# A two-layer transformer kernel: fp32 projections as three fp16 products, and feed-forward units of 256 tokens

## The chip, the cores and the metric

The kernel runs on one core of one Trainium2 chip. The metric is the time of one execution in device microseconds; the median of the runs shown stands for the kernel. All else is read from one profiled execution.

## The reference

Two layers act on x, [8, 256, 512] in fp32, so 8 batches of 256 tokens.

```python
xn = layernorm(x)
x = x + L0_attn(xn, Wqkv, Wo) + L0_ffn(xn, A, B, Wr)
xn = layernorm(x)
x = x + L1_attn(xn, Wq, bq, Wk, bk, Wv, bv) + L1_ffn(xn, gate_wq, ..., down_scale)
```

- L0_attn: 32 query heads of 16, one shared key and value head, scores with a linear bias by distance, a causal mask and softmax over 256 keys; the result times Wo (512 x 512).
- L0_ffn: four low-rank experts of rank 16; a softmax over the two largest of four gate logits mixes `xn @ A_e.T @ B_e.T`.
- L1_attn: inside each token. q is 16 x 32, k and v are 16. `scores[d, e] = sum over h of q[d, h] * k[e] * scale`, softmax over e, times v, and the 16 results are broadcast over 32 heads.
- L1_ffn: `down(silu(gate(x)) * up(x))`, 512 to 1792 to 512, with integer weights and a scale per output row.

## The kernel before

**Order.** The kernel is written step by step for each engine, and a planner in Python sets the order in which each engine meets its steps. `plan()` adds steps such as `("q", c, m)` with what they depend on; `Plan.run` simulates the engines with costs from the table `US` and takes, among the steps that could start first, the one with the lowest rank of the table `RANK` (a base and an amount per chunk). The resulting order is fixed in the program; on the chip only semaphores decide when a step starts. PSUM has eight banks in three kinds, A (2), B (4) and E (2), and each kind's banks are used in turn, so a step waits until the step that used the bank before has been read.

**Layer 0.** Tokens are taken in four chunks c of 512 (two batches i each). Per chunk: `ln0` and `xn0` normalise, `xT0` turns x by matmuls against an identity, `tok` makes keys, values and the low-rank products (fp32, 100 columns), `q` the queries in four tiles of 128x512 (fp32). ScalarE makes an fp16 high part of the queries, VectorE the low one, and both go through memory (`q_parts`) into `qq`. Then per batch: `max` (TensorE scores, VectorE maxima, 21 groups whose names carry i), `nm` (the maxima as rows of the operand), `exp` (8 head groups g of three tiles: TensorE scores, ScalarE exponentials L809 and L810, low halves by POOL L733 and VectorE L1244), `pv`, `attT` (turned attention output), `out` (Wo and the experts' second factor, five fp32 matmuls of 512 columns per 128 tokens, L983).

**Layer 1.** Per chunk of 512 tokens: `ln1`, `xn1`, `xT1` (turned x as fp16 high and low), `tok1`, the small attention `att1` to `att4` on VectorE, then 14 tiles of `gate` and `up` (8 matmuls of 512 columns each, L1014), ScalarE's tanh, VectorE's two products, the fp16 high part by ScalarE and the low by POOL (L745), and per 128 tokens `half` and `down` (28 matmuls of 512 columns, L1035).

**Side work.** POOL issues the late loads (`late`: Wo, lora_b, the weights of layer 1), and the feed-forward weights (`ffn_load`); its library call `partition_all_reduce` (L727) serves the maximum of a weight scale. SP issues the loads of x, the gathers and the stores.

The first `gate` step, behind the score groups of batch 3, divides the program: layer 0 of chunks 0 and 1 stands ahead of it, and the feed-forward fills TensorE behind it.

## Time and profile before

| | us |
|---|---|
| Median of 3 runs | 668.33 |
| Lowest and highest | 667.57, 668.47 |
| The profiled execution | 666.2 |
| Its span, first to last instruction | 664.4 |
| TensorE busy | 620.2 (93%) |
| VectorE busy | 454.2 (68%) |
| ScalarE busy | 349.8 (53%) |
| POOL busy | 284.2 (43%) |

A share is an average over stages with different limits. TensorE's mean granted clock is 0.969 of full speed. PE is TensorE, PEld its weight loads, DVE VectorE, ACT ScalarE and POOL GpSimd. An fp32 matmul leaves two records in the trace, an fp16 matmul one. Matmuls overlap, so the distance between starts tells more than the duration of one. "issue" is time in which an engine waited for nothing that the profile shows.

### The profile page before, as it was taken

The page shows a single profiled execution, that of the slowest core. Times are in us where ns is not written, and L with a number is a line of the kernel's source. Part 1 is how long each engine was busy: PE and PEld are TensorE (multiplying, and loading weights), DVE is VectorE, ACT ScalarE, POOL GpSimd, SP SyncE. Part 2 cuts the span into 40 slices and gives each one's busy share as a digit, 9 for nine tenths or more (in the row PEclk, how much of TensorE's full clock was granted, in tenths as well). Part 3 has the DMA queues.
Part 4 walks back from the last instruction along what each step waited for, and adds up shares of the span by engine and source line. Part 5 has one row for each costly group of instructions (what it writes and reads, how often), then busy time and mean ns, then how long its engine had stood idle before and what let it go on. Part 6 is the DMA issues. An engine that isn't in the chain of part 4 may idle for free.

```text
span 664.4 us, 11736 instructions
## 1 busy us (share of the span) xinstructions
PE 620.2 (93%) x4490; PEld 359.8 (54%) x4490; DVE 454.2 (68%) x936; ACT 349.8 (53%) x603; POOL 284.2 (43%) x299
## 2 busy tenths in 40 slices
PE   5989566978999999999999999999999999999997
PEld 4464444545665565565655755574654555454443
DVE  5775598984988987674668966686796554457422
ACT  3220696682558965843448748852684772023310
POOL 4203476550319773521315826632357561016310
PEclk9998685998999999999999999999999999999999
DMA  9364839466020400321103000401110000000001
GB/s 236 75 111 165 252 67 122 64 91 117 0 83 1 51 1 3 40 44 66 49 33 61 7 3 1 51 33 35 33 33 1 1 1 33 33 33 0 1 16 48
DMA packets 34567, 34.78 MB, mean 52 GB/s; under 512 B 8816, under 2 KB 24080, under 8 KB 34512
## 3 DMA queue, kind: packets, MB, share of 16 engines
q1 hardware_dynamic: 27424, 23.36, 16.6%
q0 software_dynamic: 2672, 8.36, 6.5%
q10 hardware_dynamic: 4416, 2.31, 1.3%
q8 instruction: 36, 0.59, 0.4%
q14 instruction: 19, 0.16, 0.1%
HBM read 30.15 MB, written 8.39 MB: 58 GB/s over the span
## 4 chain that ended last, share of the span: by engine, by line
PE 78%; DVE 8%; ACT 5%; issue 4%; DMA 3%; SPq 1%; POOL 0%; ACTq 0%; DVEq 0%
PE B_bank L1014 28%; PE B_bank L1035 14%; PE A_bank L983 10%; PE A_bank L900 5%; PE B_bank L922 5%; PE A_bank L954 4%; PE E_bank L938 3%; ACT probs L810 2%; DVE mx L1225 2%; ACT e L809 2%; PE A_bank L869 2%; PE B_bank L900 2%; PE E_bank L934 2%; DMA q_parts<-qs 1%; PE B_bank L1004 1%
## 5 line engine op out<-in xcount | busy, mean ns | idle before, releaser
L733 POOL TENSOR_TENSOR probs<-e,probs 128x512 f16<-128x512 f32 x128 | 153.8, 1208 | 189.4 <-ACT probs L810 179.7
L1014 PE MATMUL B_bank<-xs,wgu 128*128 128x512 f16 x896 | 200.5, 379 | 0.0
L809 ACT ACTIVATE e<-E_bank,wn 128x512 f32<-128x512 f32 x192 | 135.6, 706 | 100.1 <-PE E_bank L938 52.5
L1014 PEld LDWEIGHTS B_bank<-xs,wgu 128*128 128x128 f16 x896 | 85.4, 98 | 96.3
L810 ACT ACTIVATE probs<-E_bank,wn 128x512 f16<-128x512 f32 x192 | 135.6, 706 | 0.0
L1035 PE MATMUL B_bank<-wd,hbuf 128*128 128x512 f16 x448 | 100.3, 379 | 0.0
L1225 DVE TENSOR_REDUCE mx<-B_bank 128x8 f32<-128x256 f32 (+6 forms) x168 | 87.5, 584 | 7.2 <-PE B_bank L922 7.1
L745 POOL TENSOR_TENSOR hbuf<-hf,hbuf 128x512 f16<-128x512 f32 x56 | 67.7, 1215 | 43.7 <-ACT hbuf L836 43.6
L983 PE MATMUL A_bank<-wo_sb,attnT 128*128 128x512 f32 x160 | 71.1, 594 | 0.0
L922 PE MATMUL B_bank<-kk,qq 128*128 128x32 f16 (+20 forms) x512 | 67.4, 269 | 3.5 <-DVE mx L1225 3.2
L1035 PEld LDWEIGHTS B_bank<-wd,hbuf 128*128 128x128 f16 x448 | 43.4, 98 | 48.3
L1328 DVE SCALAR_TENSOR_TENSOR hf<-ebuf,B_bank 128x512 f32<-128x512 f32 x56 | 38.3, 684 | 42.7 <-ACT ebuf L844 35.9
L938 PE MATMUL E_bank<-qq,kk 128*128 128x256 f16 x256 | 48.0, 285 | 20.6 <-ACT probs L810 16.6
L922 PEld LDWEIGHTS B_bank<-kk,qq 128*128 128x128 f16 x512 | 57.8, 197 | 15.6 <-DVE mx L1225 8.1
L1244 DVE TENSOR_TENSOR probs<-e,probs 128x512 f16<-128x512 f32 x64 | 48.3, 755 | 13.2 <-ACT probs L810 13.1
L954 PEld LDWEIGHTS A_bank<-vv,probs 128*128 128x128 f16 x1536 | 47.9, 97 | 5.7 <-issue 1.9
L836 ACT ACTIVATE hbuf<-hf 128x512 f16<-128x512 f32 x56 | 35.4, 642 | 28.8 <-DVE hf L1335 28.6
L954 PE MATMUL A_bank<-vv,probs 128*128 128x33 f16 x1536 | 48.9, 179 | 0.9 <-DVE probs L1244 0.5
L983 PEld LDWEIGHTS A_bank<-wo_sb,attnT 128*128 128x128 f32 x160 | 29.8, 190 | 32.6 <-issue 32.0
L844 ACT ACTIVATE ebuf<-B_bank,sgx 128x512 f32<-128x512 f32 x56 | 38.9, 695 | 15.7 <-PE B_bank L1014 15.2
L1335 DVE SCALAR_TENSOR_TENSOR hf<-B_bank,sux,hf 128x512 f32<-128x512 f32 x56 | 41.8, 748 | 5.2 <-PE B_bank L1014 3.8
L938 PEld LDWEIGHTS E_bank<-qq,kk 128*128 128x128 f16 x256 | 22.1, 99 | 41.8 <-ACT probs L810 22.8
(155 smaller groups left out, 626.0 us busy)
## 6 DMA issues: line engine op xcount, KB each, us to landing
qq<-q_parts SPq DMA_DIRECT2D x21, 256.0 KB
x<-in_x SPq DMA_DIRECT2D x20, 256.0 KB, 4.3
out_y<-x SPq DMA_DIRECT2D x16, 256.0 KB, 2.0
xa<-in_x SPq DMA_DIRECT2D x12, 256.0 KB, 4.9
q_parts<-qs SPq DMA_DIRECT2D x12, 256.0 KB, 3.3
wgu<-in_gate_w POOLq DMA_DIRECT2D x4, 448.0 KB, 5.3
wgu<-in_up_w POOLq DMA_DIRECT2D x4, 448.0 KB, 5.1
wd<-in_down_w POOLq DMA_DIRECT2D x4, 448.0 KB, 7.6
```

Of the source, the lines that this page charges most:

```text
L733: pool.tensor_tensor(probs[:, u % PSLOTS, 1, :], e32[:, w, :], probs[:, u % PSLOTS, 0, :], ALU.subtract).then_inc(s_lo01, 1)
L745: pool.tensor_tensor(hbuf[:, 1, i, :], hf[:, i % 2, :], hbuf[:, 0, i, :], ALU.subtract).then_inc(s_hl, 1)
L809: act.activation(e32[:, w, :], psum("exp", i, g, w)[:, :], ACT.Exp, scale=wn[:, 7:8])
L810: act.activation(probs[:, u % PSLOTS, 0, :], psum("exp", i, g, w)[:, :], ACT.Exp, scale=wn[:, 7:8])\
L922: mm = pe.matmul(acc[:, g, :], qq[:, b, :, :].rearrange("p h (r j) -> p (h r) j", r=TR)[:, :, j], keys.rearrange("p t k -> p (t k)")[:, 0: ...
L938: mm = pe.matmul(acc[:, :, j0:j0 + JT // 2], kk[:, b, half, w, :], tokens[:, :, w // 2 * JT + j0:w // 2 * JT + j0 + JT // 2], start=True, ...
L954: mm = pe.matmul(pvb[:, qt, j, :], probs[:, (3 * n + w) % PSLOTS, part, j * P:(j + 1) * P], vv[:, c % 2, 2 * b + kt, :], start=(kt == 0 an ...
L983: mm = pe.matmul(psum("out", i, t)[:, :], attnT[:, k, t * P:(t + 1) * P], wo_sb[:, k, :], start=(k == 0), stop=(k == NK))
L1014: mm = pe.matmul(psum(name, c, i)[:, :].rearrange("p (t n) -> p t n", t=NT), wgu[:, m, k, i * P:(i + 1) * P], xs[:, :, part, k, :], start= ...
L1035: mm = pe.matmul(psum("half", c, t)[:, :], hbuf[:, part, i, t * P:(t + 1) * P], wd[:, i, :], start=(i == 0 and part == 0), stop=(i == NI - ...
L1225: dve.tensor_reduce(mx[:, i % 2, j0:j0 + count], psum("max", i, n)[:, 0:count * width].rearrange("p (g k) -> p g k", g=count), AX.X, ALU.m ...
L1244: dve.tensor_tensor(probs[:, u % PSLOTS, 1, :], e32[:, w, :], probs[:, u % PSLOTS, 0, :], ALU.subtract).then_inc(s_lo2, 1)
```

## The change

- The products of `out`, for all chunks, and of `q` and `tok`, for chunks 1 to 3, are made of fp16 pairs. Each operand is split into a high and a low part, and three products (high by high, high by low, low by high) are added in PSUM: 12 fp16 matmuls for a `q` tile in place of 4 fp32, 24 of 100 columns for `tok` in place of 8, 14 for `out` in place of 5 (the experts' two parts stand in one operand). Chunk 0's `q` and `tok` stay fp32.
- The weights are loaded as fp32 into `hbuf`, scaled and split: `squares2` (ScalarE), `norm2` (POOL, a second `partition_all_reduce`), `scale2` (VectorE, 15 small instructions), `hi` (POOL, ten) and `lo` (VectorE, ten). VectorE has a new low part for each turned tile of x (`xT0`, chunks 1 to 3) and of attention (`attT`), and `mixb` makes both parts of `midz`.
- The feed-forward goes in eight units u of 256 tokens. Two column blocks of `gate` or `up` share a PSUM bank: 16 matmuls of 256 columns for a pair. The tanh and `up`'s product, whose scale differs by block, are two instructions of 256 columns. The down product is in four steps of 4, 4, 4 and 2 tiles. `hbuf`, the small attention's scratch and the like are doubled by unit, and layer 1's steps come per unit.
- `US`, `RANK` and the dependences are new; `q` and `out` are issued in two halves (`qa`, `q`; `outa`, `out`).

```diff
+PAIRS = ((0, 0), (0, 1), (1, 0))
...
-    "PE": {"xT0": (25.5, 4), "tok": (-3.5, -1), "kT": (-12.5, -2), "q": (0.5, 4), "norm": (-25.5, 4), "max": (7, 1), "exp": (7, 2),
+    "PE": {"xT0": (31, 0.5), "tok": (16.5, 3), "kT": (-3, 0.5), "qa": (81.5, -2), "q": (33.5, 2), "norm": (19.5, 0), "max": (3.5, 0),
...
+        p.add("PE", ("outa", i, t), sp("x1_load", 2 * i + t, gap=0.0), dve("attT", i, 0), dve("attT", i, 1), act("midT", i),
+              *([dve("lo", 9)] if i == 0 else []))
+        p.add("PE", ("out", i, t), pe("outa", i, t, gap=0.0))
+        p.add("DVE", ("out", i, t), pe("out", i, t), sp("x1_load", 2 * i + t))
...
+def feed_forward(p, u):
+        p.add("PE", ("gate", u, i), *(first if i == 0 else []))
+        p.add("PE", ("up", u, i), pe("gate", u, i, gap=0.0))
+        n = NPR * u + i - 2
+        p.add("ACT", ("gate", u, i), pe("gate", u, i), *([dve("gate", n // NPR, n % NPR)] if n >= 0 else [dve("setup3")]))
+        p.add("DVE", ("gate", u, i), act("gate", u, i), *([pool("up", n // NPR, n % NPR)] if n >= 0 else []))
+        p.add("DVE", ("up", u, i), pe("up", u, i), dve("gate", u, i), *([dve("att4", u)] if i == (NI - 5) // 2 else []))
+        p.add("ACT", ("up", u, i), dve("up", u, i))
+        p.add("POOL", ("up", u, i), act("up", u, i))
...
+        p.add("PE", ("half", u, t), pool("up", u, 1), *([pe("up", u, NPR - 1, gap=0.0)] if t == 0 else [pe("down", u, t - 1, gap=0.0)]))
+        p.add("PE", ("half2", u, t), pe("half", u, t, gap=0.0), pool("up", u, 3))
+        p.add("PE", ("half3", u, t), pe("half2", u, t, gap=0.0), pool("up", u, 5))
+        p.add("PE", ("down", u, t), pe("half3", u, t, gap=0.0), pool("up", u, NPR - 1))
+        p.add("DVE", ("down", u, t), pe("down", u, t), pool("att4", u), *([dve("down", u, t - 1)] if t else [dve("down", u - 1, NU - 1)] if u else []))
+        p.add("SP", ("down", u, t), dve("down", u, t))
...
+                p.add("ACT", ("squares2", n), *([pool("late", n + 1, gap=6.0), pool("late", 4, gap=6.0)] if n else [act("squares", NK - 1)]))
+            p.add("POOL", ("norm2",), act("squares2", 2))
+            p.add("DVE", ("scale2",), pool("norm2"), dve("scale"))
+            for n in range(10):
+                p.add("POOL", ("hi", n), dve("scale2"), *([pool("clear")] if n == 9 else []))
...
+            def norm2():
+                pool.wait_ge(s_sq2, 3)
+                pool.partition_all_reduce(wm[:, 0:3], wsq2[:, :], P, bass.bass_isa.ReduceOp.add).then_inc(s_n2b, 1)
+                pool.wait_ge(s_n2b, 1)
+                pool.tensor_scalar(wm[:, 0:3], wm[:, 0:3], 1.0 / NORM ** 2, 1e-30, ALU.mult, ALU.max).then_inc(s_n2c, 1)
+                pool.wait_ge(s_n2c, 1)
...
+            def hi(n):
+                if n == 0:
+                    pool.wait_ge(s_scale2, 1)
+                if n < NK:
+                    high = pool.tensor_scalar(wq2[:, n, 0, :], wq_sb[:, n, :], wm[:, 15:16], None, ALU.mult)
+                elif n == NK:
+                    pool.tensor_scalar(wtok2[:, :, 0, 0:C_L], wtok[:, :, 0:C_L], wm[:, 15:16], None, ALU.mult)
+                    high = pool.tensor_scalar(wtok2[:, :, 0, C_L:TOKC], wtok[:, :, C_L:TOKC], wm[:, 16:17], None, ALU.mult)
+                else:
+                    col = 10 if n < 2 * NK + 1 else 11
+                    high = pool.tensor_scalar(wo2[:, n - NK - 1, 0, :], wo_sb[:, n - NK - 1, :], wm[:, col:col + 1], None, ALU.mult)
...
+            def lo(n):
...
+                    last = low(wq2[:, n, 1, :], wq_sb[:, n, :], wm[:, 15:16], wq2[:, n, 0, :])
...
+            def xT0(c, t):
+                dve.wait_ge(s_xTh, NT * (c - 1) + t + 1)
+                dve.scalar_tensor_tensor(out=xp[:, t, 1, :, :].rearrange("p k n -> p (k n)"), in0=psum("xT0", c, t)[:, :], scalar=XS,
+                                         in1=xp[:, t, 0, :, :].rearrange("p k n -> p (k n)"), op0=ALU.mult,
+                                         op1=ALU.subtract).then_inc(free("xT0", c, t), 1)
...
+                            for n, (xpart, wpart) in enumerate(PAIRS):
+                                mm = pe.matmul(acc, xp[:, 2 * w + t, xpart, k, :], wtok2[:, k, wpart, :],
+                                               start=(k == 0 and n == 0), stop=(k == NK - 1 and n == 2))
...
+                        for n, (wpart, xpart) in enumerate(PAIRS):
+                            mm = pe.matmul(acc, wq2[:, k, wpart, m * P:(m + 1) * P], xp[:, :, xpart, k, :],
+                                           start=(k == 0 and n == 0), stop=(k == NK - 1 and n == 2))
...
+                    for n, (apart, wpart) in enumerate(PAIRS if k < NK else PAIRS[0:2]):
+                        tokens = attnT[:, apart, k, t * P:(t + 1) * P] if k < NK else midT[:, t * P:(t + 1) * P]
+                        mm = pe.matmul(psum("out", i, t)[:, :], tokens, wo2[:, k, wpart, :],
+                                       start=(k == 0 and n == 0), stop=(k == NK and n == 1))
...
+            def gate_or_up(name, u, i, m):
+                t0 = NU * u % NT
+                wait_free(pe, name, u, i)
+                for a in range(2):
+                    for k in range(NK):
+                        for part in (0, 1):
+                            mm = pe.matmul(psum(name, u, i)[:, a * SEQ:(a + 1) * SEQ].rearrange("p (t n) -> p t n", t=NU),
+                                           wgu[:, m, k, (2 * i + a) * P:(2 * i + a + 1) * P], xs[:, t0:t0 + NU, part, k, :],
+                                           start=(k == 0 and part == 0), stop=(k == NK - 1 and part == 1))
+                mm.then_inc(full(name, u, i), 1)
...
+                for a in range(2):
+                    sig = act.activation(ebuf[:, n % 2, a * SEQ:(a + 1) * SEQ], psum("gate", u, i)[:, a * SEQ:(a + 1) * SEQ], ACT.Tanh,
+                                         scale=sgx[:, 2 * i + a:2 * i + a + 1])
```

TensorE, before, from the end of chunk 0's preparation to the start of the scores `max(0)` (L900 is `q`, L858 `xT0`, L869 `tok`, L922 `max`):

```order
L900 MATMUL B_bank<-xa,wq_sb 128x512 x8
L858 MATMUL A_bank<-identf,xa 128x128 x16
L869 MATMUL A_bank<-wtok,xa 128x100 x16
L900 MATMUL A_bank<-xa,wq_sb 128x512 x4
L922 MATMUL B_bank<-kk,qq 128x32 x8
L922 MATMUL B_bank<-kk,qq 128x64 x8
L922 MATMUL B_bank<-kk,qq 128x84 x5
```

And now (L999 is `q` of chunk 0, L992 `kT`, L954 `xT0`, L1038 `max`):

```order
L969 MATMUL B_bank<-hbuf,xa 128x100 x8
L999 MATMUL B_bank<-xa,hbuf 128x512 x16
L992 MATMUL A_bank<-identh,kc 56x128 x4
L954 MATMUL A_bank<-identf,xa 128x128 x16
L1038 MATMUL B_bank<-kk,qq 128x32 x8
L1038 MATMUL B_bank<-kk,qq 128x64 x8
L1038 MATMUL B_bank<-kk,qq 128x84 x5
```

`tok(1)` and the first `q` tile of chunk 1 no longer stand ahead of `max(0)`.

TensorE, before, behind `max(0)`, where chunk 1's other three `q` tiles stand (L938 and L934 are `exp`):

```order
L922 MATMUL B_bank<-kk,qq 128x252 x2
L922 MATMUL B_bank<-kk,qq 128x256
L900 MATMUL A_bank<-xa,wq_sb 128x512 x12
L938 MATMUL E_bank<-qq,kk 128x16x16 x2
L934 MATMUL E_bank<-qq,kk 128x512
```

And now, far on in `exp(0)` (L1054 and L1050 are `exp`, L1002 `q` of chunks 1 to 3, L1070 `pv`), since nearly all of `max(1)` has come first:

```order
L1054 MATMUL E_bank<-qq,kk 128x16x16 x2
L1002 MATMUL A_bank<-xa,wq 128x512 x6
L1054 MATMUL E_bank<-qq,kk 128x16x16 x2
L1050 MATMUL E_bank<-qq,kk 128x512
L1002 MATMUL A_bank<-xa,wq 128x512 x6
L1054 MATMUL E_bank<-qq,kk 128x16x16 x2
L1002 MATMUL A_bank<-xa,wq 128x512 x6
L1054 MATMUL E_bank<-qq,kk 128x16x16 x2
L1002 MATMUL A_bank<-xa,wq 128x512 x18
L1070 MATMUL A_bank<-vv,probs 128x33 x24
```

Chunk 1's `q` moved from one block between `max(0)` and `exp(0)` to pieces between groups of `exp(0)`.

POOL, before, from its all-reduce (L727) to its first low halves (L733):

```order
L727 ISA
L727 ISA cmax<-cmax 128x1
L703 DMA wo_sb<-in_wo 128x4x512
L703 DMA wo_sb<-in_lora_b 64x512
L703 DMA xs<-in_wq 128x4x512
...
L703 DMA dsb<-in_down_s 128x512
L733 ISA
L733 TENSOR_TENSOR probs<-e,probs 128x512 x2
```

And now, from the load of Wo (L752 is the all-reduce of `norm2`, L754 and L756 its steps, L762 a `hi`, L808 an `exp` low):

```order
L778 DMA hbuf<-in_wo 128x4x512
L778 DMA hbuf<-in_lora_b 64x512 x2
L752 ISA
L752 ISA wm<-wsq 128x3
L754 ISA
L754 TENSOR_SCALAR wm<-wm 128x3
L756 TENSOR_TENSOR wm<-wm,mhalf 128x3
L778 DMA xs<-in_wq 128x4x512
...
L778 DMA dsb<-in_down_s 128x512
L808 TENSOR_TENSOR probs<-e,probs 128x512 x2
L762 TENSOR_SCALAR wq<-hbuf,wm 128x512
```

The all-reduce of `norm2` and its arithmetic stand between the load of Wo and the loads of layer 1.

VectorE, now, in the middle of `max(1)` (L1422): `scale2` is L1218 to L1232, `mixb(0)` ends at L1387, L1441 is an `exp` low:

```order
L1422 TENSOR_REDUCE mx<-B_bank 128x3 x4
L1422 TENSOR_REDUCE mx<-B_bank 128x2 x2
L1218 TENSOR_SCALAR wm<-wm 128x3
L1219 SCALAR_TENSOR_TENSOR wm<-wm 128x3
...
L1232 COPY wm<-wm 128x1
L1422 TENSOR_REDUCE mx<-B_bank 128x2
L1372 SCALAR_TENSOR_TENSOR gate<-grk,gex 128x16
...
L1422 TENSOR_REDUCE mx<-B_bank 128x2 x8
L1422 TENSOR_REDUCE mx<-B_bank 128x1
L1441 TENSOR_TENSOR probs<-e,probs 128x512
L1238 SCALAR_TENSOR_TENSOR wq<-hbuf,wm,wq 128x512
```

Before, `mixb(0)` came ahead of `max(0)`, and `scale2` did not exist.

## Rows read from the trace of the kernel before

**Rows 1.** The page, part 2: busy tenths and granted clock in 40 slices.

```profile
PE   5989566978999999999999999999999999999997
...
PEclk9998685998999999999999999999999999999999
```

**Rows 2.** Windows: length, busy (xcount) of PE, PEld, DVE, ACT, POOL; clock, DMA, GB/s.

```profile
0.00:46.24 46.24, 36.11 (x171) 24.07 (x172) 30.76 (x98) 13.59 (x29) 12.45 (x30) 1.00 0.64 143
46.24:187.41 141.17, 114.80 (x937) 74.96 (x937) 109.61 (x241) 78.62 (x137) 64.39 (x75) 0.85 0.54 106
187.41:664.40 476.99, 469.30 (x3386) 260.73 (x3384) 313.81 (x598) 257.58 (x437) 207.36 (x194) 1.00 0.12 28
190.45:664.40 473.95, 466.26 (x3346) 258.45 (x3341) 312.70 (x596) 256.36 (x436) 207.36 (x194) 1.00 0.12 27
```

**Rows 3.** Groups of VectorE by form, 46.24 to 187.41 us: busy, mean ns, idle before.

```profile
L1153 DVE SCALAR_TENSOR_TENSOR qs<-A_bank,wn,qs 128x256 f16<-128x256 f32 x13 | 5.7, 480 | 17.7 <-ACT qs L783 17.7
...
L1274 DVE SCALAR_TENSOR_TENSOR xs<-B_bank,xs 128x512 f16<-128x512 f32 x4 | 2.6, 683 | 0.0
```

**Rows 4.** Timeline of TensorE: start, us, instruction, xcount [idle before].

```profile
190.45 1.89 PE L1014 MATMUL B_bank<-xs,wgu 128*128 128x512 f16 x8
...
250.79 4.46 PE L983 MATMUL A_bank<-wo_sb,attnT 128*128 128x512 f32 x10
255.08 0.38 PE L934 MATMUL E_bank<-qq,kk 128*128 128x512 f16 x1
...
269.53 3.61 PE L1014 MATMUL B_bank<-xs,wgu 128*128 128x512 f16 x16
272.98 0.60 PE L938 MATMUL E_bank<-qq,kk 128*128 128x256 f16 x4
273.41 0.60 PE L858 MATMUL A_bank<-identf,xa 128*128 128x128 f32 x4
...
282.09 1.16 PE L1004 MATMUL B_bank<-w,xs 128*128 128x144 bf16 x16
283.08 0.38 PE L938 MATMUL E_bank<-qq,kk 128*128 128x256 f16 x2
...
328.17 3.71 PE L869 MATMUL A_bank<-wtok,xa 128*128 128x100 f32 x32
331.72 0.38 PE L938 MATMUL E_bank<-qq,kk 128*128 128x256 f16 x2
...
337.10 3.60 PE L900 MATMUL A_bank<-xa,wq_sb 128*128 128x512 f32 x8
340.53 0.76 PE L954 MATMUL A_bank<-vv,probs 128*128 128x33 f16 x24
```

**Rows 5.** The page, part 5: groups of three engines.

```profile
L733 POOL TENSOR_TENSOR probs<-e,probs 128x512 f16<-128x512 f32 x128 | 153.8, 1208 | 189.4 <-ACT probs L810 179.7
...
L1014 PEld LDWEIGHTS B_bank<-xs,wgu 128*128 128x128 f16 x896 | 85.4, 98 | 96.3
...
L810 ACT ACTIVATE probs<-E_bank,wn 128x512 f16<-128x512 f32 x192 | 135.6, 706 | 0.0
```

**Rows 6.** Timeline of GpSimd, 26 to 77 us.

```profile
26.26 0.38 POOL L727 PARTITION_ALL_REDUCE cmax<-cmax  x1 [5.27 <-issue]
...
51.14 0.94 POOL L703 DMA_DIRECT2D wo_sb<-in_wo  x1 [24.50 <-DMA qq<-q_parts]
...
74.86 2.26 POOL L733 TENSOR_TENSOR probs<-e,probs 128x512 f16<-128x512 f32 x2 [9.45 <-issue]
```

**Rows 7.** DMA issues up to 110 us: count, KB each, median us to landing.

```profile
wo_sb<-in_wo POOLq DMA_DIRECT2D x1, 1024.0 KB, 5.6
```

**Rows 8.** Timeline of VectorE: a small instruction, and the last reduction's start.

```profile
19.88 0.16 DVE L1075 TENSOR_TENSOR wn<-wn 128x1 f32<-128x1 f32 x1
...
660.33 0.69 DVE L1346 TENSOR_TENSOR hf<-B_bank,dsb 128x512 f32<-128x512 f32 x1 [4.63 <-PE B_bank L1035]
```

**Rows 9.** Groups of VectorE by form, whole span.

```profile
L1316 DVE TENSOR_TENSOR hbuf<-hbuf,t 128x1024 f32<-128x1024 f32 x4 | 7.4, 1845 | 0.1
```

More of the change, by code:

```diff
@@ L1019, in gate_ @@
[L1019 to L1035 removed]
+                mm.then_inc(full("tok1", u), 1)
@@ new lines, in half2, with half3, down @@
+            def half2(u, t):
+                down_tiles(u, t, range(4, 8))
+            def half3(u, t):
+                down_tiles(u, t, range(8, 12))
+            def down(u, t):
+                down_tiles(u, t, range(12, NI)).then_inc(full("down", u, t), 1)
+            run("PE", {"xT0": xT0, "norm": norm, "tok": tok, "kT": kT, "qa": qa, "q": q, "max": max_, "exp": exp, "pv": pv, "attT": attT, "midT": turn_mid, "outa": outa, "out": out_,
+                 "xT1": xT1, "tok1": tok1, "gate": gate_, "up": up, "half": half, "half2": half2, "half3": half3, "down": down})
```

685 lines of the change are left out of this document (390 added, 295 removed), and 9 rows, old and new, of tables (RANK, US).

## Prediction

> **What bounds the kernel now.** I read the slices of the span first, then the busy time by stage, then the pitch of each kind of matmul in TensorE's timeline. The slices show TensorE at 9 tenths in most of the span and at 5 to 8 in slices 5 to 10, where the granted clock is low too [rows 1]. The stages say why [rows 2]. The cut at 46.24 us is the first score reduction (`max`) on VectorE; the one at 187.41 us is the end of the score groups `max(3)`; at 190.45 us the first `gate` tile of the feed-forward begins. From there to the end TensorE is busy 466.26 of 473.95 us at clock 1.00: this stage is as long as its matmuls. From 46.24 to 187.41 us it is busy 114.80 of 141.17 at clock 0.85, and VectorE 109.61: here neither is full, and VectorE, which must reduce the scores, add the low halves of the probabilities and close each head group, sets the pace wherever it doesn't itself wait. Its largest wait there is 17.7 us for ScalarE's `qs` [rows 3], which stands for the `q` tiles of the next chunk that TensorE makes in one block.
>
> **What the change removes from TensorE.** Prices are starts to next starts [rows 4]. An fp32 matmul leaves two records.
> - `out`: ten records, one tile of five fp32 matmuls, 250.79 to 255.08, 4.29 us. The fp16 price: 16 of 128x512 from 269.53 to 272.98, 0.2157 each; now 14 of them, 3.02 us. Saved 1.27 a tile, 16 tiles: 20.3 us.
> - `q`: one tile of four fp32 matmuls 337.10 to 340.53, 3.43 us; now 12 x 0.2157 = 2.59. Saved 0.84, for the 12 tiles of chunks 1 to 3: 10.1 us.
> - `tok`: two in 328.17 to 331.72, 1.775 each; now 24 fp16 matmuls of 100 columns. No row has that shape. The nearest, 16 of 144 columns with a weight load each, took 282.09 to 283.08, 0.062 each: 1.5 us as the dear bound, and 0.043 each by columns, 1.04, as the cheap one. I take 1.07, since 144-column matmuls run at the rate of their columns. Saved 0.7 x 6 = 4.2 (bounds 1.7 and 4.4).
> - Feed-forward: 8 matmuls of 512 columns (1.726) become 16 of 256. Four of 256 took 272.98 to 273.41, 0.108 each, but in a scattered place, and the weight load takes 98 ns [rows 5], 10 ns under that. Taken at 0.109: 1.744, +0.018 on each of 112 pairs: +2 us in all with the down tiles' edges. Bounds: 0 and the 98 ns load not fully hidden, say 5 ns x 1792 = 9 us.
> Sum: about 34.6 - 2 = 32.6 us of TensorE work. Of it 12 `out` tiles, one chunk of `q` (4 tiles) and of `tok` (2) lie behind the first `gate`: 15.2 + 3.4 + 1.4 - 2 = 18 us. The other 14.6 us lie ahead of it, where TensorE has 26 us of idle time already: they gain only as far as VectorE lets them.
>
> The Trainium skill (TensorE: Matmul & The Clock Gate, "Back-to-back issue gap") speaks against this change. It says that in a sustained stream of weight load and matmul pairs 128 columns take about 81 ns each, and 512 about 131. The trace disagrees with both: 144 columns at 62 ns, 512 at 215.7. By that rule smaller matmuls lose part of what they save; it is rival E below.
>
> **Behind the gate.** 473.95 us includes the tail, in which the last reduction starts at 660.33 [rows 8], 4.1 us before the end; without it 469.9. Minus 18: 451.9. VectorE carries more there: its 313 us of work become about 335 (lows of `xT0` and `attT`, two `up` instructions where one was, layer-1 attention in eight smaller parts). Against 452 it doesn't bind, but there are more handovers in two PSUM banks of kind A; I double TensorE's idle time of 3.6 us that isn't tail. So 456 us from the first gate to the last down tile.
>
> **Ahead of the gate.** The order shows the first `gate` right behind `max(3)` in both, with 19 and 20 of the head groups of `exp` done. So I sum VectorE's list between `max(0)` and `max(3)`. Before: 109.6. Added:
> - 11 lows of the weights, 4 of `xT0`, 4 of `attT`: 19 x 0.66, near the 0.683 of the like instruction L1274 [rows 3]: 12.6.
> - `scale2`: 15 tiny instructions at 0.16 to 0.18 [rows 8]: 2.6.
> - `mixb(0)` now behind `max(0)`, with two more for `midz`: 3.0. `tok(1)` and `q(1,0)` moved behind it: 3.0.
> - Layer-1 attention of unit 0, whose place was later: half of five passes over 1024 columns, the longest of which took 1.85 [rows 9]: 4.5.
> - Less `ln1`, `xn1` and `xT1` for two tiles rather than four: -3.5.
> Together 132 us. It starts at about 44.5, not 46.24: TensorE no longer has `tok(1)` and a `q` tile ahead of it (5 us), VectorE has four lows more (2.7).
>
> Now its stalls. The main new one is `scale2`, which stands in the middle of `max(1)` and can't be passed. It waits for POOL's `norm2`, and that for the squares of Wo. Wo is issued at 51.14 [rows 6] behind the gather of the first query rows; with the new order of the queues 1.5 later is my guess, 52.7, and one more load is issued behind it (lora_b twice, 0.5 us); it lands 5.6 us after issue [rows 7], 58.5; ScalarE's squares over 2048 and 512 columns take less than five times the 0.706 of a 512-column instruction [rows 5], 2.8, so 61.3; the all-reduce 0.4; then POOL must go back to its ordinary code. Before the first all-reduce POOL shows 5.27 us of issue, and 9.45 us after it, before its first `exp` low, while the DMA engines are full [rows 6]. With 5.3: 67, and two small steps on POOL and the wakeup: 68.2. VectorE gets there after 12 groups of `max(1)`, at 61.5. So 6.7 us of idle; with 9.45 it is 11. Behind it `max(1)`'s other nine groups and hence `exp(0)`'s first lows queue, and TensorE's `max(1)`, whose four banks aren't freed. In exchange the 9.45 of before, which held up `exp(0)` at 65 to 75 us, isn't paid again, since the return comes earlier.
> Other bubbles: the 17.7 us behind `qs` should mostly go, because `q(1)` is now spread between `exp` groups in blocks of 6 instead of standing in one block of 12 fp32 matmuls; I keep 8 us. POOL in `exp(0)` has 16 lows of 1.208 [rows 5] and, at the same price, 10 highs of the weights: 31 us, beside ScalarE's 48 exponentials at up to 0.706, 34. About level, so I give it nothing; if POOL's loads of the feed-forward weights come between, some 3 us. TensorE runs 2 us ahead of VectorE at the end of `max(3)`.
> First gate: 44.5 + 132 + 6.7 + 8 - 2 = 189, against 190.45: almost nothing of the 14.6 us comes out here, since VectorE takes in 22 us more work.
>
> **The sum.** 189 + 456 = 645, tail 4.1: span 649.3. The profiled execution of before was 666.2, 1.8 over its span: 651.1. The median, 668.33, is 2.1 over that: **653 us**, 2.3% faster.
>
> **The rivals.**
> - *The stage ahead is not held up* (B). VectorE's bubbles are all filled: gate at 44.5 + 132 - 2 = 174.5, so 639. For it: the new ranks interleave three kinds of work, and TensorE's 100 us leave it room. Against: `scale2` waits for a load. 0.15.
> - *VectorE idles half as much again* (C): 22.7 instead of 14.7, by 9.45 for the code return and slow `q` blocks: gate at 197, 661. 0.14.
> - *Slower* (D). One mechanism: the new list on VectorE keeps the share of idle time of before, 31.6 of 141.2, 22.4%, because each new low (ScalarE's high, then VectorE's low, then TensorE) is one more handover in a chain. 132/0.776 = 170: gate at 212.6, 677. It decides from a gate at about 204.5, which is 31 us of idle time. Against: 17.7 of those 31.6 have one cause that the order removes. 0.08.
> - *The small matmuls don't run at the rate of their columns* (E). A 98 ns load beside 0.109 leaves 11 ns. If a quarter of each load shows, +25 ns on 1792 matmuls, 45 us, it would be 698; break-even at +9 ns on each. The 62 ns at 144 columns, loads and all, speak against it. 0.02. The page of the Trainium skill named above has the same 25 ns between its figure for a stream of pairs and its 56 ns for a 128-column matmul alone.
> - *No change* within 0.2% (what a measurement of this kernel can tell from none): 0.03, where a late gate meets the gain behind it.
>
> **How the numbers follow.** The forecast case (646 to 659) has 0.58: its width is the 8 us of bubbles and the 3.6 of extra idle time, either way. The range 641 to 665 leaves out most of D and E and part of B. Faster 0.87 (forecast, B, C), same 0.03, slower 0.10.
>
> **What would show it.** Of before's kinds: `out` tiles at 3.0 us, `q` at 2.6 and pairs at 1.74 in the timeline (a pair of 2.1 is E). Busy TensorE time from the first gate about 448. The first gate at 189: below 180 is B, over 200 is D. VectorE idle ahead of `scale2` for 5 to 9 us, POOL's second return from the all-reduce at about 5 us, and VectorE's list between 44.5 and the gate at 132. I would be wrong if POOL's highs hold `exp(0)` and with it `q(1)`, or if the layer-1 ops, twice as many at half size, cost much more than half each and VectorE becomes the bound behind the gate.

## The result, and the profile after

The changed kernel took 674.74 us (median of six runs, 671.63 at the lowest), the one before 667.95 beside it: a ratio of 1.0099, 95% interval 1.0067 to 1.0131. Two disturbed executions, one of the changed kernel at 2,680 us and one of the kernel before at 684 us, are left out of the ratio. The change makes the kernel 1.0% slower, and the forecast was 2.3% faster. The profiled execution was 675.78 us, its span 674.0, 9.6 us over the span of before.

The page of the changed kernel, parts 1 and 2 (busy time; busy tenths and granted clock in 40 slices), beside [rows 1]:

```profile
PE 603.1 (89%) x5546; PEld 435.5 (65%) x5546; DVE 516.4 (77%) x1106; ACT 362.6 (54%) x669; POOL 307.2 (46%) x313
...
PE   4968267767799999999999999999999999999997
...
PEclk9976558779989999998999999999999999999999
```

Slices 4 to 12 hold the stage ahead of the feed-forward: TensorE is at 6 to 7 tenths in most of them and at 2 in slice 5 (67 to 84 us), at clock 0.5 to 0.7 in slices 3 to 6. The windows of the changed kernel, cut at the first score reduction on VectorE (46.72 us) and at the first `gate` tile, as in [rows 2]:

```profile
0.00:46.72 46.72, 32.79 (x121) 21.97 (x122) 28.54 (x86) 13.47 (x30) 11.84 (x29) 0.95 0.60 137
46.72:206.93 160.21, 116.40 (x1092) 75.12 (x1092) 139.62 (x300) 84.06 (x146) 87.86 (x90) 0.78 0.52 104
206.93:674.00 467.07, 453.88 (x4336) 338.42 (x4336) 348.28 (x722) 265.10 (x494) 207.48 (x194) 1.00 0.13 26
```

The first `gate` stands at 206.93 us, 16.5 later than before's 190.45. Behind it the kernel takes 467.07 us, 6.9 less than before's 473.95. So the feed-forward side gained, and the stage ahead lost more than twice that.

The prices of TensorE's work, from its timeline in the changed kernel (start, us, instruction), answer to [rows 4]:

```profile
153.35 2.76 PE L1097 MATMUL A_bank<-wo,attnT 128*128 128x512 f16 x12 [0.16 <-DVE xa L1253]
155.95 0.59 PE L1097 MATMUL A_bank<-wo,midT 128*128 128x512 f16 x2
156.38 0.90 PE L1038 MATMUL B_bank<-kk,qq 128*128 128x236 f16 x7
...
159.51 2.75 PE L1002 MATMUL A_bank<-xa,wq 128*128 128x512 f16 x12
162.10 0.38 PE L1054 MATMUL E_bank<-qq,kk 128*128 128x256 f16 x2
...
181.48 1.24 PE L972 MATMUL A_bank<-wtok,xa 128*128 128x100 f16 x24 [0.39 <-ACT kk L884]
182.55 0.38 PE L1050 MATMUL E_bank<-qq,kk 128*128 128x512 f16 x1
...
206.93 1.91 PE L1145 MATMUL B_bank<-xs,wgu 128*128 128x256 f16 x16 [0.29 <-DVE mx L1422]
208.68 0.38 PE L1054 MATMUL E_bank<-qq,kk 128*128 128x256 f16 x2
```

Start to start, an `out` tile is 3.03 us (forecast 3.02), a `q` tile 2.59 (2.59), a `tok` 1.07 (1.07), and sixteen 256-column matmuls 1.75 (1.744). Every price of a matmul in the forecast held. What did not hold is the stage ahead of the gate. Its largest single wait stands in the timelines of the three other engines around the second all-reduce, first GpSimd:

```profile
53.44 0.94 POOL L778 DMA_DIRECT2D hbuf<-in_wo  x1 [13.00 <-DMA qq<-q_parts]
54.40 1.10 POOL L778 DMA_DIRECT2D hbuf<-in_lora_b  x2
64.04 0.43 POOL L752 PARTITION_ALL_REDUCE wm<-wsq  x1 [8.54 <-ACT wo L854]
71.79 0.29 POOL L754 TENSOR_SCALAR wm<-wm 128x3 f32<-128x3 f32 x1 [7.32 <-issue]
```

then ScalarE's squares of Wo, which waited for the load, and VectorE:

```profile
61.29 1.91 ACT L854 ACTIVATE wo<-hbuf 128x2048 f16<-128x2048 f32 x1 [17.11 <-DMA hbuf<-in_lora_b]
```
```profile
46.72 0.42 DVE L1422 TENSOR_REDUCE mx<-B_bank 128x8 f32<-128x256 f32 x1 [1.82 <-PE B_bank L1038]
...
58.27 5.16 DVE L1422 TENSOR_REDUCE mx<-B_bank 128x8 f32<-128x512 f32 x10
73.11 0.17 DVE L1218 TENSOR_SCALAR wm<-wm 128x3 f32<-128x3 f32 x1 [9.68 <-POOL wm L756]
```

and TensorE, whose scores wait for the banks that VectorE hasn't read:

```profile
75.70 0.61 PE L1038 MATMUL B_bank<-kk,qq 128*128 128x220 f16 x2 [8.83 <-DVE mx L1422]
```

The load is issued at 53.44 and 54.40 and lands by 61.29; the squares end at 64; the all-reduce is followed by 7.32 us in which GpSimd waits for nothing that the profile shows; VectorE, ready at 63.4, begins `scale2` at 73.11.

### The profile page after: what moved, and what is told of

Read it like the earlier page. It is cut to its first block, busy times and chain, and to the rows that moved or that the text cites. A ratio compares the mean times of both kernels' runs of the same rounds, so it can differ in the third digit from the quotient of the medians.

```text
span 674.0 us, 14126 instructions
## 1 busy us (share of the span) xinstructions
PE 603.1 (89%) x5546; PEld 435.5 (65%) x5546; DVE 516.4 (77%) x1106; ACT 362.6 (54%) x669; POOL 307.2 (46%) x313
## 4 chain that ended last, share of the span: by engine, by line
PE 40%; DVE 13%; issue 2%; ACT 1%; POOL 0%; DVEq 0%; ACTq 0%
PE B_bank L1145 19%; PE B_bank L1166 12%; DVE mx L1422 4%; PE A_bank L1097 2%; PE A_bank L1070 2%; DVE probs L1441 2%; PE E_bank L1054 1%; DVE hf L1541 1%; PE B_bank L1120 1%; PE A_bank L1002 1%; DVE osum L1449 1%; PE E_bank L1050 1%; PE B_bank L1133 1%; DVE hf L1531 1%; DVE attn L1457 0%
## 5 line engine op out<-in xcount | busy, mean ns | idle before, releaser
L808 POOL TENSOR_TENSOR probs<-e,probs 128x512 f16<-128x512 f32 x128 | 156.3, 1226 | 136.5 <-ACT probs L901 136.1
L1145 PE MATMUL B_bank<-xs,wgu 128*128 128x256 f16 x1792 | 206.1, 273 | 0.4 <-DVE mx L1422 0.3
L1145 PEld LDWEIGHTS B_bank<-xs,wgu 128*128 128x128 f16 x1792 | 173.8, 98 | 23.7 <-DVE mx L1422 1.0
L900 ACT ACTIVATE e<-E_bank,wn 128x512 f32<-128x512 f32 x192 | 133.9, 698 | 76.7 <-DVE probs L1441 28.4
L901 ACT ACTIVATE probs<-E_bank,wn 128x512 f16<-128x512 f32 x192 | 133.9, 697 | 0.0
L1422 DVE TENSOR_REDUCE mx<-B_bank 128x8 f32<-128x256 f32 (+6 forms) x168 | 87.9, 582 | 6.8 <-PE B_bank L1038 6.6
L1038 PE MATMUL B_bank<-kk,qq 128*128 128x32 f16 (+20 forms) x512 | 68.0, 280 | 18.0 <-DVE mx L1422 9.3
L1038 PEld LDWEIGHTS B_bank<-kk,qq 128*128 128x128 f16 x512 | 57.0, 195 | 29.3 <-DVE mx L1422 15.7
L939 ACT ACTIVATE ebuf<-B_bank,sgx 128x256 f32<-128x256 f32 x112 | 47.3, 478 | 51.2 <-PE B_bank L1145 49.1
L1070 PEld LDWEIGHTS A_bank<-vv,probs 128*128 128x128 f16 x1536 | 46.5, 97 | 20.2 <-issue 11.8
L1054 PE MATMUL E_bank<-qq,kk 128*128 128x256 f16 x256 | 51.8, 290 | 8.7 <-ACT probs L901 8.3
L1070 PE MATMUL A_bank<-vv,probs 128*128 128x33 f16 x1536 | 48.4, 179 | 12.0 <-DVE probs L1441 6.1
L1441 DVE TENSOR_TENSOR probs<-e,probs 128x512 f16<-128x512 f32 x64 | 55.5, 867 | 2.1 <-ACT probs L901 1.8
L1541 DVE SCALAR_TENSOR_TENSOR hf<-B_bank,sux,hf 128x256 f32<-128x256 f32 x112 | 48.7, 477 | 9.9 <-PE B_bank L1145 9.7
L1097 PE MATMUL A_bank<-wo,attnT 128*128 128x512 f16 x192 | 46.0, 379 | 0.2 <-DVE xa L1253 0.2
L1551 DVE TENSOR_TENSOR ytmp<-B_bank,dsb 128x512 f32<-128x512 f32 x16 | 11.0, 690 | 40.8 <-PE B_bank L1166 40.8
L1054 PEld LDWEIGHTS E_bank<-qq,kk 128*128 128x128 f16 x256 | 21.9, 101 | 26.0 <-ACT probs L901 14.5
```

The source lines that it names most:

```text
L808: pool.tensor_tensor(probs[:, u % PSLOTS, 1, :], e32[:, w, :], probs[:, u % PSLOTS, 0, :], ALU.subtract).then_inc(s_lo01, 1)
L900: act.activation(e32[:, w, :], psum("exp", i, g, w)[:, :], ACT.Exp, scale=wn[:, 7:8])
L901: act.activation(probs[:, u % PSLOTS, 0, :], psum("exp", i, g, w)[:, :], ACT.Exp, scale=wn[:, 7:8])\
L1038: mm = pe.matmul(acc[:, g, :], qq[:, b, :, :].rearrange("p h (r j) -> p (h r) j", r=TR)[:, :, j], keys.rearrange("p t k -> p (t k)")[:, 0: ...
L1054: mm = pe.matmul(acc[:, :, j0:j0 + JT // 2], kk[:, b, half, w, :], tokens[:, :, w // 2 * JT + j0:w // 2 * JT + j0 + JT // 2], start=True, ...
L1070: mm = pe.matmul(pvb[:, qt, j, :], probs[:, (3 * n + w) % PSLOTS, part, j * P:(j + 1) * P], vv[:, c % 2, 2 * b + kt, :], start=(kt == 0 an ...
```

## The experiments

Each run was timed in five rounds against the kernel before on the same chip; ratios are to the kernel before, with their 95% interval. "Work" of an engine in a stretch is the sum from each start to the next start less the idle time shown between, over the rows of its timeline; "idle" is the rest. "Gate" is the start of the first `gate` tile. All of these are read from one profiled execution, while the executions of one kernel differ by 2.5 to 7.5 us. early_wo and one_instruction_a_bank (2 and 7 below) are the same program up to the gate, and their profiles differ by 0.9 us at the gate and by 1.5 at the first score reduction; so a difference of a us or two between two gates shows nothing.

**1. no_allreduce.** The second all-reduce is a copy, so that no library call stands there. Each partition then scales by its own sums alone, and the scales are not the reference's.

```
-                pool.partition_all_reduce(wm[:, 0:3], wsq2[:, :], P, bass.bass_isa.ReduceOp.add).then_inc(s_n2b, 1)
+                pool.tensor_copy(wm[:, 0:3], wsq2[:, :]).then_inc(s_n2b, 1)
```

> The second partition_all_reduce is left out: each partition's own sums of squares stand in its place, so the scales of Wo and of the experts' weights are not the reference's. Theory 1 (scale2 waits on POOL's return from the all-reduce): the 7.32 us of issue behind it and its 0.43 us go, VectorE waits for scale2 some 2 us where it waited 9.68, the first gate comes 7.7 us earlier, at about 199, and the kernel takes 0.989 of the changed one. Theory 2 (VectorE and POOL have too much work behind it, and the wait only orders it): the gate moves by under 3 us, ratio over 0.996.

Measured: 665.55 us, 0.9968 [0.9946, 0.999]. The timeline of GpSimd in it:

```profile
61.41 0.19 POOL L752 COPY wm<-wsq 128x3 f32<-128x3 f32 x1 [8.00 <-ACT wo L854]
61.69 0.29 POOL L754 TENSOR_SCALAR wm<-wm 128x3 f32<-128x3 f32 x1
```

The 7.32 us of issue are gone, and with them VectorE's wait (0.4 us is left). The gate comes at 197.03, 9.9 earlier than in the changed kernel (7.7 were expected), and the time is 0.987 of the changed kernel's by the two ratios (0.989 was expected). The return from the all-reduce, from its end to GpSimd's next instruction, is a real delay on the path.

**2. early_wo.** ScalarE's queue issues Wo and the two halves of `lora_b` at the start; GpSimd no longer issues them behind the gather.

```
             def late(n):
-                if n == 2:
-                    pool.wait_ge(s_gather[0], 16 * 3 * NK)
-                    pool.wait_ge(s_gather[1], 16 * 3)
+                if 2 <= n < 5:
+                    return
...
                 act.dma_start(tri_sb[:, :, :], tri).then_inc(s_tri, 16)
+                for dst, source, loaded in late_loads[2:5]:
+                    act.dma_start(dst, source).then_inc(loaded, 16)
```

> Wo and both copies of lora_b are issued by ScalarE right behind the other layer 0 weights rather than by POOL behind the first gathers. Theory 1 (the chain load, squares, all-reduce, return to ordinary code is what is late): the chain ends before VectorE reaches scale2, its whole 9.68 us of wait go, first gate at 196 to 198, 0.986 of the changed kernel. Theory 2: gate moves by under 3 us. A third way: 1.3 MB more in the first 15 us delays the loads of x and wq, and the start of max(0) goes from 46.7 to 50, which eats a third of the gain.

Measured: 663.86 us, 0.9948 [0.9921, 0.9975]: faster than the kernel before, and by the two ratios 1.5% faster than the changed one (0.9948/1.0099 = 0.985). GpSimd's timeline, VectorE's, and the windows about the gate:

```profile
46.93 0.43 POOL L752 PARTITION_ALL_REDUCE wm<-wsq  x1 [6.54 <-ACT wo L855]
54.61 0.29 POOL L754 TENSOR_SCALAR wm<-wm 128x3 f32<-128x3 f32 x1 [7.25 <-issue]
```
```profile
63.61 0.29 DVE L1219 TENSOR_SCALAR wm<-wm 128x3 f32<-128x3 f32 x1
```
```profile
46.00:194.89 148.89, 114.03 (x1101) 73.90 (x1102) 138.68 (x300) 82.60 (x146) 86.06 (x87) 0.84 0.52 102
194.89:662.00 467.11, 454.49 (x4336) 338.78 (x4336) 348.24 (x722) 265.47 (x494) 207.49 (x194) 0.99 0.13 26
```

The return still takes 7.25 us, but it ends 9 us ahead of VectorE's need, and `scale2` (a line lower here, L1219) has no wait at all. The gate comes at 194.89, 12.0 earlier; the stage behind is the same to 0.1 us. So one wait of 9.68 us cost 12.0 us in these profiles. The granted clock of the stage went from 0.78 to 0.84 with the wait gone; that this makes the 2.3 us between the two numbers, and not the difference between any two profiles, is an argument, not shown.

**3. hi_on_act and ffn_units_alone.** In the first the planner was told to put the high halves of the weights on ScalarE; in the second the feed-forward units stayed and the projections went back to fp32, with the planner's costs and dependencies changed to match.

```
-                p.add("POOL", ("hi", n), dve("scale2"), *([pool("clear")] if n == 9 else []))
-                p.add("DVE", ("lo", n), pool("hi", n))
+                p.add("ACT", ("hi", n), dve("scale2"), *([pool("clear")] if n == 9 else []))
+                p.add("DVE", ("lo", n), act("hi", n))
```
```
-                    for n, (apart, wpart) in enumerate(PAIRS if k < NK else PAIRS[0:2]):
...
+                    mm = pe.matmul(psum("out", i, t)[:, :], attnT[:, k, t * P:(t + 1) * P], wo_sb[:, k, :],
```

> The ten high parts of the weights are made by ScalarE rather than POOL. Theory 2a (VectorE instructions whose operands all lie in SBUF are held up while POOL works on SBUF: the 11 lows of weights took 13.0 us where 0.7 each was forecast, POOL's highs up to 2.1 each): POOL loses 16 us of work, the lows take under 9 us together, VectorE is busy 4 us less ahead of the gate, the gate comes 4 to 6 us earlier, 0.992. Theory 1 (only the wait for scale2 counts): the gate moves by under 1.5 us. If ScalarE becomes the limit of exp(0), it gets later by 3 us or more.

> The projections are fp32 as before, with their weights in place from the start and no split; the feed-forward in units of 256, its two column blocks to a bank and the changed tables stay. If the units are neutral but for 2.7 us of TensorE work, it takes 1.004 of the kernel before (0.994 of the changed one), with the first gate near 190 to 193. If the units cost by themselves (twice as many small VectorE and ScalarE instructions behind the gate), 1.010 or more of the kernel before and TensorE idle more than 12 us behind the gate. If they gain, under 0.998 of it, and then the projections cost all of the loss and more.

Measured: 687.07 us, 1.0283 [1.025, 1.0315], and 688.31, 1.0313 [1.0282, 1.0343]. Both miss everything that was expected, and neither says anything about its edit: the planner, with the ranks tuned for another list, wrote a different order for the whole program. In the second the gate came early, at 184.96, with two `out` tiles and a `q` tile more left behind it (14 and 5, not 12 and 4), and the stage behind took 503 us, 36 more than the changed kernel's. Experiment 5 has the same fp32 projections in the changed kernel's order and takes 673.0 us; the 15 us between the two are the order's, so every later run fixes the order of the steps.

**4. hi_act_fixed.** early_wo, and the highs on ScalarE with no other step moved: each stands in ScalarE's list at the planned time that it had in GpSimd's.

```
+_moved = [e for e in ORDER["POOL"] if e[1][0] == "hi"]
+ORDER["POOL"] = [e for e in ORDER["POOL"] if e[1][0] != "hi"]
+for _t, _s in _moved:
+    _at = min(n for n, e in enumerate(ORDER["ACT"]) if e[0] > _t)
+    ORDER["ACT"].insert(_at, (_t, _s))
```

> As early_wo, with the ten high parts of the weights on ScalarE, put into its list by their planned times; no other step changes its place (hi_on_act let the planner move everything else, which hid the answer). Theory 2a (POOL's work on SBUF holds up VectorE's instructions whose operands lie in SBUF, and the other way round): POOL has 16 us less, the 11 lows go from 12.0 us of VectorE's time to 8 or 9, the other exp lows and attn products get shorter too, the first gate comes at 189 to 191 rather than 194.9, ratio 0.986 to 0.990 of the kernel before where early_wo had 0.9948. Rival: ScalarE, which is in the chain of every exp group, gets 6 us more and the gate comes no earlier or later, 0.994 or more.

Measured: 661.9 us, 0.9915 [0.9887, 0.9942], its interval overlapping that of early_wo. Now the durations of VectorE's `low` of the weights, first in the changed kernel and then here (ns: min/median/max):

```profile
L1238 DVE SCALAR_TENSOR_TENSOR wo<-hbuf,wm,wo x5: 739/1634/1642, 111.3 to 120.8; 128x512 f16<-128x512 f32 x4, 64x512 f16<-64x512 f32 x1
L1238 DVE SCALAR_TENSOR_TENSOR wq<-hbuf,wm,wq x4: 747/747/3378, 87.0 to 91.8; 128x512 f16<-128x512 f32 x4
```
```profile
L1244 DVE SCALAR_TENSOR_TENSOR wo<-hbuf,wm,wo x5: 740/747/1641, 101.0 to 111.3; 128x512 f16<-128x512 f32 x4, 64x512 f16<-64x512 f32 x1
L1244 DVE SCALAR_TENSOR_TENSOR wq<-hbuf,wm,wq x4: 744/747/1152, 77.2 to 84.2; 128x512 f16<-128x512 f32 x4
```

The same instruction takes 0.74 us or 1.6 or 3.4, and it is slow less often with GpSimd relieved. VectorE's work ahead of the gate fell from 141.6 us (early_wo) to 133.9. But its idle time rose from 6.5 to 14.9 (4.6 of it for ScalarE's `qs`), and the gate came at 196.11, no earlier: neither the 189 to 191 nor the ratio of at most 0.990 that was expected. The profiled execution, at 664.59 us, was the slowest of the six, whose median is 661.9, so whether the gate usually comes earlier than in early_wo is open. In this profile, what was taken off VectorE came back as waits.

**5. fp32_same_order.** The changed kernel's order, step by step, with the projections in fp32: no splitting, no second norm, no lows. Wo is loaded where it was.

```
-                    for n, (apart, wpart) in enumerate(PAIRS if k < NK else PAIRS[0:2]):
...
+                    mm = pe.matmul(psum("out", i, t)[:, :], attnT[:, k, t * P:(t + 1) * P], wo_sb[:, k, :],
+                                   start=(k == 0), stop=(k == NK))
```

> The changed kernel with its own order of steps, word for word, but all projections in fp32 again: no weights' split, no second norm, no lows for xT0 and attT. If the products earn behind the gate what the pitches say (15 us there), TensorE's work behind the gate goes from 455 to 471 us and the stretch from 467 to about 482; ahead of it the 9.7 us wait and 26 us of VectorE work go, TensorE gets 15 us back: first gate at about 192; together 677, 1.013 of the kernel before. If the loss of the changed kernel comes from the products' preparation alone, it is at or under the kernel before (0.995 to 1.003).

Measured: 673.0 us, 1.0088 [1.0065, 1.0112]. Its windows:

```profile
46.00:189.31 143.31, 125.19 (x1004) 81.27 (x1002) 113.22 (x261) 82.40 (x141) 66.21 (x75) 0.87 0.56 114
189.31:669.70 480.39, 470.96 (x4258) 347.21 (x4256) 336.77 (x702) 267.54 (x495) 207.65 (x194) 0.99 0.12 25
```

This kernel splits the change in two. In the profiles, against the one before, the new order and the units move the gate by 1.1 us (190.45 to 189.31) and make the stage behind 6.4 us longer (473.95 to 480.39). Adding the products then costs 17.6 us ahead of the gate and earns 13.3 behind it. -1.1 + 6.4 + 17.6 - 13.3 = 9.6, the whole difference of the spans. And of the 17.6, early_wo gives back 12.0: the rest of the splitting costs 5.6.

The ratios, which rest on all runs, weigh the two parts otherwise. The order and the units alone are at 1.0088, the changed kernel at 1.0099: nearly the whole loss is theirs, and what the products cost and earn cancels within the noise. With the load early (0.9948 in the same order) the products gain 1.4%. The expectation that the loss comes from the products' preparation alone is refuted.

**6. products_in_old_order, products_old_order_2, out_only_old_order.** The order and the 512-token feed-forward of before, with products put in: all `out` tiles, and `q` and `tok` of chunks 2 and 3; Wo early, `norm2` behind the first all-reduce, `scale2` behind `max(0)`, highs on ScalarE. The second issues Wo behind `kT(1)` rather than at the start, since the load at the start made the first keys late. The third keeps `q` and `tok` in fp32.

```
+put("POOL", ("setup1",), ("norm2",))
+put("DVE", ("nm", 0), ("scale2",), ("mids", 0))
+put("ACT", ("q", 1, 1), ("hi", 0), ("hi", 1))
...
+put("DVE", ("q", 1, 1), ("lo", 0), ("lo", 1))
```

> The kernel before, with its order of steps, its fp32 q and tok for chunk 1 and its feed-forward in chunks of 512; out for all chunks and q and tok of chunks 2 and 3 are fp16 products. Wo is loaded by ScalarE at the start, norm2 stands right behind the first all-reduce, scale2 behind max(0), the highs are made by ScalarE and the lows by VectorE between chunk 1's q tiles, where both waited (19.6 us). TensorE's work behind the gate goes from 467 to 448, the stretch from 474 to 456; VectorE gets 17 us more ahead of the gate, of which 10 or so fit into its 31 us of waits: first gate at 190 to 197, 0.970 to 0.983 of the kernel before. Rival: none of the new work fits into waits, the gate comes at 205, 0.993 or more.

> As products_in_old_order, but ScalarE issues Wo and lora_b behind kT(1), at about 28 us, and not at the start, where they put back max(0) from 44.5 to 52.0 us. Theory 3 (the early megabyte delays the constants that kT needs): max(0) starts at 44 to 46 again, the first gate comes at 190 to 192 rather than 197.7, 0.979 to 0.984 of the kernel before. Rival: VectorE's list ahead of the gate is full anyway and the gate comes at 195 or later, 0.988 or more.

> As products_old_order_2, but q and tok stay fp32 in all chunks: only Wo and lora_b are split. TensorE gets back 6.7 + 2.8 us of work (3.4 + 1.4 of them behind the gate); VectorE loses six lows of weights and eight of xT0, 9 us, 5.5 of them ahead of the gate and the others in a stretch where TensorE waits 11.8 us, mostly for VectorE. If VectorE's small additions are what eats the products' gain, it is as fast as products_old_order_2 or faster by up to 0.4%; if TensorE's work counts, 0.5% slower.

Measured: 660.73 us, 0.9908 [0.9876, 0.9941]; 662.49, 0.9922 [0.9895, 0.9948]; 662.06, 0.991 [0.9874, 0.9947]. All three beat both kernels, and they can't be told from one another. None reaches what was expected of the first two (0.970 to 0.983, and 0.979 to 0.984). The windows of the second and the third:

```profile
46.00:193.89 147.89, 114.76 (x1053) 76.87 (x1052) 125.31 (x283) 87.41 (x151) 63.32 (x75) 0.84 0.52 96
193.89:659.70 465.81, 449.81 (x3426) 249.83 (x3422) 326.80 (x615) 255.44 (x436) 208.13 (x194) 1.00 0.13 28
```
```profile
46.00:189.84 143.84, 118.54 (x1022) 79.98 (x1021) 121.51 (x273) 83.83 (x145) 64.14 (x75) 0.86 0.54 102
189.84:657.80 467.96, 455.42 (x3394) 253.93 (x3389) 324.92 (x612) 255.63 (x436) 208.12 (x194) 0.99 0.13 28
```

In the first the gate came at 197.67 with `max(0)` at 51.95 on TensorE: in that profile the early megabyte did cost, and the second brought `max(0)` back to 47.51 and the gate to 193.89. The medians don't show it: the second is no faster than the first, whose profiled execution, at 665.59 us, was the slowest of its six. Behind the gate of the first TensorE's work without the tail was 450.2 us, close to the 448 expected, but its idle time 11.8, and the stage took 466 rather than 456. The second and third bear on what `q` and `tok` products are worth: they spare TensorE 5.6 us of work behind the gate (450.4 against 456.0), of which 3.6 come back as idle time (11.4 against 7.8), and they cost 4 us ahead of it.

The lows of the weights in products_in_old_order, at times at which GpSimd only issues DMAs or is idle (but for the last 0.08 us of one of its products):

```profile
L1200 DVE SCALAR_TENSOR_TENSOR wo<-hbuf,wm,wo x5: 737/747/753, 102.2 to 104.8; 128x512 f16<-128x512 f32 x4, 64x512 f16<-64x512 f32 x1
L1200 DVE SCALAR_TENSOR_TENSOR wq<-hbuf,wm,wq x4: 741/744/747, 68.2 to 72.2; 128x512 f16<-128x512 f32 x4
```

All nine are at 0.74 to 0.75 us.

**7. one_instruction_a_bank.** early_wo, with one `tanh` and one `up` product over each 512-column bank in place of two over 256. The odd block of a pair gets the even block's scale, so its values are not the reference's.

```
-                for a in range(2):
-                    sig = act.activation(ebuf[:, n % 2, a * SEQ:(a + 1) * SEQ], psum("gate", u, i)[:, a * SEQ:(a + 1) * SEQ], ACT.Tanh,
-                                         scale=sgx[:, 2 * i + a:2 * i + a + 1])
+                sig = act.activation(ebuf[:, n % 2, :], psum("gate", u, i)[:, :], ACT.Tanh, scale=sgx[:, 2 * i:2 * i + 1])
```

> early_wo with one tanh and one up product of 512 columns to a bank, both with the scale of the even block, so the odd blocks' values are not the reference's. VectorE has 7 us less behind the gate (112 x 0.477 becomes 56 x 0.75 or so), ScalarE 8. My forecast's doubled idle time of TensorE behind the gate put this among its causes: if it is one, TensorE's idle time there falls from 7.6 us by 2 or more, 0.991 of the kernel before where early_wo had 0.9948. If the two short instructions cost nothing because both engines have room there, 0.994 to 0.996.

Measured: 663.67 us, 0.9947 [0.9924, 0.997], the same as early_wo. ScalarE was busy 8.9 us less and VectorE 4.3 less over the span, and TensorE's idle time behind the gate stayed at 7.3 us (7.2). The doubled tanh and `up` products are not what idles TensorE there.

## Why the prediction was wrong

**Right.** The price of each matmul; that the 256-column ones run at the rate of their columns. Behind the gate TensorE's `out` fell from 51.57 to 36.65 us, `q` from 13.79 to 10.58 and `tok` from 3.55 to 2.43: 19.2 us, where 20.0 were forecast. The rival in which small matmuls run slower is refuted: behind the gate gate and up take 0.1097 us per matmul of 256 columns (196.6 us for 1,792, short waits between them included), and 0.1094 in the rows above. The Trainium skill (TensorE: Matmul & The Clock Gate, "Back-to-back issue gap") gives streams of weight load and matmul another price than the columns', about 131 ns at 512 columns and 81 at 128. The trace does not agree: 215.7 ns at 512 columns [rows 4], and 256 columns take about half of that.

**The step that failed** is the sum for the first gate, "44.5 + 132 + 6.7 + 8 - 2 = 189". Its list runs to the end of `max(3)`, which came at 209.96 us. Measured by the same terms it was 46.7 + 145.4 + 9.7 + 8.2 - 3.0 = 207, 18 us more:
- VectorE's list: 145.4 against "Together 132 us" (+13.4); up to the gate itself it is 142.5. The 11 weight lows took 12.5 us (1.04 each by their starts) against 7.3; the last part of a layer-1 weight operand (L1406; the same line before took 0.4) took 3.2; the lows of `exp` 12.8 against 11.8. Those are 9 of the 13.4. Another 2 are short gaps between instructions: the forecast began from before's busy time, 109.6, where start to next start gives 111.7. The error is in a choice: "19 x 0.66, near the 0.683 of the like instruction L1274". L1274 reads one input from PSUM; a weight low reads both from SBUF, and such an instruction was held up in the rows of the last section. The lows of `xT0` and `attT`, which read PSUM, did come out at 0.62 to 0.63.
- "So 6.7 us of idle": 9.68 (+3.0). The load was issued at 53.44 rather than 52.7 and had landed at 61.29 rather than 58.5, 7.9 us after its issue and not 5.6 (lora_b's two halves are part of it). The return took 7.32 us rather than 5.3, between the two ends that the forecast named. Together `scale2` began 4.9 us later than forecast, at a VectorE that itself got there 1.9 later.
- The other bubbles were 8.2 (8). The number is right by luck: the 8 were kept for what would be left of the waits for `qs`, and those shrank from 19.6 us to 0.2; 4.3 of the 8.2 are waits for the scores of `max`, 1.7 for `attnT`.
- The start was 2.2 late, and TensorE's lead was 3.0 and not 2.

The same sum put to the kernel before would have warned: 46.2 + 109.6 + 31.6 - 2 = 185.4, where its gate stood at 190.45, since there the gate came 3 us behind the end of `max(3)` and not ahead of it.

How much each part is worth, the runs show for the wait alone: without it (early_wo) the gate comes 12.0 earlier. But the forecast had counted 6.7 for it, and without a wait its sum gives 182.5, where early_wo has 194.89. So the wait makes 5 of the 18 us, and the 12 that are left stand in early_wo too: 144.4 of list rather than 132, a start 2.5 later, less 1.5 of bubbles and 1.0 of lead. The mis-sized list is the larger part of the error, the wait the part that could be edited away.

What a us of added work costs is not settled. From the first score reduction to the gate it is 144 us with 112.9 of work on VectorE (before), 144 with 116.5 (fp32_same_order), 144 and 145 with 126.6 and 126.9 (the first two of experiment 6), 149 with 133.9 (hi_act_fixed) and 148 with 141.6 (early_wo): twenty-nine us more on VectorE lengthen the stage by four, while its waits shrink from 31.4 to 6.5. The third of experiment 6 speaks against it: with 3.6 us less work than the second its stage is 4.3 shorter (140 with 123.3), at the same idle time. And in early_wo the waits are nearly used up, 6.5 us of 148. A sum of one engine's list and a guessed number of bubbles doesn't tell when added work fills a wait and when it doesn't; that this is a fault of the method beside the wrong price is an argument from these rows, not shown by an edit.

**The rivals.** The slower one (D) came true in its outcome, a gate beyond 204.5, and not in its mechanism: it had VectorE idle for 22% of the stage, and it idled 11%, 17.9 us and so less than C's 22.7. The longer list did most of it.

**Behind the gate** 467.07 us against 460.1 with the tail, +7.0. TensorE's work fell by 11.6 us (466.9 to 455.3) rather than 18. The step "Minus 18" lacked three things: two tiles of `xT1` and `tok1` moved behind the gate (1.6); gate and up tiles came to +3.2 rather than +2; and 3.2 us on the scores and probabilities, in whose starts to next starts short waits may be hidden; `out`, `q` and `tok` were 0.8 short of their sum, and the fp16 transposes of `midz` gave 0.7 back. TensorE's idle time went from 2.9 to 7.6, where "I double TensorE's idle time" gave 3.6 of extra. fp32_same_order puts a 6.4 us loss in this stage on the order and the units. That the doubled tanh and `up` products cause the idle time is excluded by experiment 7; which of the other halved steps, or which step's place, costs the 6.4 us is not settled.

## What to carry to other kernels

In a stage in which several engines wait on each other, ask first which new event everything queues behind, trace that chain back to the load that starts it, and issue the load early; here that one edit turned +1.0% into -0.5%. Put a sum for a stage to the kernel before first, and see whether it gives the time that is known. Price an added instruction by a row that reads its inputs from the same memory, beside the same neighbour engine, and compare two versions of a planned kernel only with the order of steps held fixed. Faster matmuls for one projection could not be told from faster matmuls for all three (0.991 and 0.992): in the profiles the 5.6 us of TensorE's work that the other two spared went in idle time (3.6) and in a later gate (4).
